# Gram lower triangles: four tiles loaded at once, two late, and the stores issued by ScalarE

## What is computed

```python
Z = jnp.einsum('bnd,bmd->bnm', inputs, inputs)
li, lj = jnp.tril_indices(64, k=-1)
return Z[:, li, lj]
```

## Time and profile before

| | before |
|---|---|
| median of 3 runs | 429.29 us |
| the profiled run | 430.24 us |
| its span | 428.5 us |
| TensorE matmul busy | 379.3 us |
| VectorE busy | 365.0 us |
| ScalarE busy | 177.9 us |
| GpSimd busy | 197.3 us |
| DMA, share of 16 engines' span | 92.8% |
| bytes read and written in HBM | 134.22 + 16.52 MB |
| mean granted TensorE clock | 0.979 |

### The profile page before, as it was taken

The page is one execution under the profiler, slowest core; times in us unless marked ns, Lnnn a source line. Parts: engine busy times, 40 slices in busy tenths (PEclk is TensorE's granted clock), DMA queues, the critical chain, the costliest instruction groups (busy, mean ns, idle before and its releaser), DMA issues.

```text
span 428.5 us, 68861 instructions
## 1 busy us (share of the span) xinstructions
PE 379.3 (89%) x33024; PEld 372.2 (87%) x33024; DVE 365.0 (85%) x224; ACT 177.9 (42%) x829; POOL 197.3 (46%) x980
## 2 busy tenths in 40 slices
PE   3529999999999999999999999999999998989900
PEld 3529999999999999999999999999999998989800
DVE  5316799999999999999999999999897979979734
ACT  0001213455335543455344543455444554344562
POOL 0000037281827465472808347182744728173584
PEclk9999999999999999999999999999999999999965
DMA  6699999999999999999999999999999999995416
GB/s 227 255 401 413 382 348 357 365 330 401 398 390 412 368 414 401 410 388 406 405 407 389 394 398 342 401 350 384 371 411 361 370 409 361 398 350 226 107 37 157
DMA packets 39610, 151.01 MB, mean 352 GB/s; under 512 B 4640, under 2 KB 4768, under 8 KB 39584
## 3 DMA queue, kind: packets, MB, share of 16 engines
q1 hardware_dynamic: 39584, 150.75, 92.8%
HBM read 134.22 MB, written 16.52 MB: 352 GB/s over the span
## 4 chain that ended last, share of the span: by engine, by line
PE 72%; SPq 11%; issue 6%; DMA 4%; POOL 3%; DVE 2%; ACT 0%; DVEq 0%; POOLq 0%; ACTq 0%
PE bank_set L264 72%; SPq L146 10%; DMA y_dram<-packed_rows 4%; POOL packed_rows L130 3%; SPq L151 1%; DVE packed_rows L130 1%; DVE row_halves L225 1%; DVE x_turned L231 0%; ACT products L291 0%; ACT packed_rows L125 0%; DVEq L67 0%; SPq L157 0%; DVEq L224 0%; POOLq L187 0%; ACTq L282 0%
## 5 line engine op out<-in xcount | busy, mean ns | idle before, releaser
L264 PE MATMUL bank_set<-x_turned 32*64 32x64 f32 x33024 | 379.3, 236 | 28.7 <-issue 18.2
L264 PEld LDWEIGHTS bank_set<-x_turned 32*64 32x64 f32 x33024 | 372.2, 132 | 35.6 <-issue 28.1
L208 DVE STREAM_TRANSPOSE x_turned<-x_in 128x2048 f32<-128x2048 f32 x128 | 292.0, 2290 | 49.2 <-PE bank_set L264 29.5
L130 POOL COPY packed_rows<-row_halves 32x60 f32<-32x60 f32 (+30 forms) x961 | 195.0, 205 | 224.7 <-DVE row_halves L225 100.2
L291 ACT COPY products<-bank_set 128x512 f32<-128x512 f32 (+1 forms) x91 | 68.6, 759 | 211.9 <-PE bank_set L264 192.5
L225 DVE STREAM_TRANSPOSE row_halves<-products 128x1024 f32<-128x1024 f32 x64 | 76.9, 1205 | 6.9 <-POOL packed_rows L130 5.3
L119 ACT COPY packed_rows<-row_halves 128x32 f32<-128x32 f32 (+30 forms) x481 | 62.8, 220 | 0.0
L125 ACT COPY packed_rows<-row_halves 128x128 f32<-128x128 f32 x256 | 57.0, 301 | 10.0 <-DMA y_dram<-packed_rows 7.8
L291 ACT ACT_TABLE_LOAD x1 | 1.3, 1283 | 20.6 <-PE bank_set L264 20.6
L130 DVE COPY packed_rows<-row_halves 32x2 f32<-32x2 f32 (+30 forms) x31 | 3.5, 191 | 0.0
L231 DVE MEMSET x_turned<- 128x2048 f32 x1 | 1.8, 1765 | 1.2 <-PEq L335 1.2
## 6 DMA issues: line engine op xcount, KB each, us to landing
x_in<-x_dram SPq DMA_DIRECT2D x256, 512.0 KB, 7.5
y_dram<-packed_rows SPq DMA_DIRECT2D x30, 504.0 KB, 7.3
y_dram<-packed_rows SPq DMA_DIRECT2D x2, 380.0 KB, 3.9
y_dram<-packed_rows SPq DMA_DIRECT2D x2, 124.0 KB, 3.9
```

The lines of the kernel that those rows point to most:

```text
L130: return copy(packed_rows[first:first + BLOCK, group % 2, :, at + BLOCK:at + i], row_halves[first + BLOCK:first + HALF, i, :, 0:i - BLOCK])
L208: nc.vector.transpose(x_turned[:, j].rearrange("p s c b (h u n v) -> p u v (s c b h) n", h=ROWS // BLOCK, u=PAIRS, v=PAIR), x_in[:, k].rea ...
L264: done = nc.tensor.matmul(bank_sets[s][side * HALF:(side + 1) * HALF, g, at, :].rearrange("r (n u v) -> r u n v", u=PAIRS, v=PAIR), rows, ...
```

## The change

Four edits:

1. Tiles 0 to 3 load without waits. Tile 4 waits until tile 0 has been multiplied, tile 5 until tile 1 has been. Tiles 6 and 7 follow in the queue, and from 8 on it is as before.
2. The stores of groups 0 to 14 are issued by ScalarE instead of SyncE: in the loop after a `keep`, once all 16 quarters of the group are packed, with the same waits; for group 14 after the loop, ahead of the first quarter of group 15. The two stores of group 15 stay with SyncE.
3. TensorE waits for the other set's `kept` ahead of the last two chunks of the last tile of each set: the wait for `kept[1]` moves from the start of `j` = 2 to near the end of `j` = 1. The wait for `kept[0]` stays where it was.
4. The tile of zeros is cleared half by VectorE (side 0), half by GpSimd (side 1).

```diff
-    APART = range(2, 5)
+    LATE = {4: 0, 5: 1}
@@ store, now with the engine as an argument
+        def store(engine, group, columns):
+            for side in range(SIDES):
+                first = group * GROUP + side * KEPT
+                engine.dma_start(y[first:first + KEPT, columns].rearrange("(h q) c -> q h c", q=BLOCK),
+                                 packed_rows[side * HALF:side * HALF + BLOCK, group % 2, :, columns]).then_inc(
+                    stored[group % 2], 16)
@@ sync
-                elif t in APART:
-
-                    sync.wait_ge(loaded[t - 1], SIDES * 16)
+                elif t in LATE:
+                    lap, j = place(LATE[t])
+                    sync.wait_ge(tile_multiplied[j], (lap + 1) * ARRAY_TILES)
...
             for t in range(TILES):
                 load(t)
-                group, behind = divmod(t - STORE_LAG, GROUP_TILES)
-                if group >= 0 and behind == 0:
-                    store_whole(group)
-            for group in range((TILES - 1 - STORE_LAG) // GROUP_TILES + 1, GROUPS - 1):
-                store_whole(group)
@@ gpsimd
             pool.sem_inc(kept[1], LAP)
+            for j in range(BLANK):
+                nc.gpsimd.memset(x_turned[:, j, 1:SIDES], 0.0).then_inc(turned[j], LAP - 1)
@@ vector
-                nc.vector.memset(x_turned[:, j], 0.0).then_inc(turned[j], LAP)
+                nc.vector.memset(x_turned[:, j, 0:1], 0.0).then_inc(turned[j], 1)
@@ tensor
                 s, in_set = set_of(j)
-                if s == 1 and in_set == 0:
-                    pe.wait_ge(kept[1], step)
...
-                        if j == LAP - 1 and slot == SLOTS - 1 and c == CHUNKS - 2:
-
-                            pe.wait_ge(kept[0], step)
+                        if in_set == SET_TILES[s] - 1 and slot == SLOTS - 1 and c == CHUNKS - 2:
+
+                            pe.wait_ge(kept[1 - s], step)
@@ scalar
+            def store_whole(group):
+                act.wait_ge(packed_home, (group + 1) * PIECES)
+                act.wait_ge(packed_across, (group + 1) * LONG_PIECES)
+                store(act, group, slice(0, PACKED))
+
             n = 0
+            stores = 0
             for lap in range(LAPS):
                 for s in range(SETS):
                     keep(lap, s)
+                    if n >= (stores + 1) * PIECES * 4:
+                        store_whole(stores)
+                        stores += 1
                     while n + PACK_LAG < (lap * LAP + (SET_TILES[0] if s == 0 else LAP) - BLANK) * 2:
                         pack(n)
                         n += 1
 
             for n in range(n, (GROUPS * PIECES - 1) * 4):
+                if n == (GROUPS - 1) * PIECES * 4:
+                    store_whole(GROUPS - 2)
                 pack(n)
```

More of the change, by code:

```diff
@@ L60, in gram_lower_triangle @@
     PACK_LAG = 2 * PIECE_LAG + 1
-    STORE_LAG = PIECE_LAG + 2 * PIECES + 3 + IN_RING
     STORES = SIDES * 16
@@ L171, in _ @@
             sync.wait_ge(last_carried, 1)
-            store(group, slice(long_rows, PACKED))
+            store(sync, group, slice(long_rows, PACKED))
             sync.wait_ge(packed_home, GROUPS * PIECES - 1)
             sync.wait_ge(last_packed, 1)
-            store(group, slice(0, long_rows))
+            store(sync, group, slice(0, long_rows))
             for b in range(2):
```

## The result

| | before | after |
|---|---|---|
| median | 428.72 us | 421.80 us (420.55 to 422.23) |
| ratio, 95% interval | | 0.9851 (0.9814 to 0.9889) |
| span of the profiled run | 428.5 us | 418.7 us |

The forecast was 424.0 us, 1.2% faster, in a range of 416 to 431.

The account below looks back on a forecast made before the run. The prediction took the DMA stream of loads and stores to bound the kernel from store 0 on. Span 428.5 less 1.4 (TensorE's end) and 3.9 (tail) gave 423.2, scaled to 424.0 us, range 416 to 431.

Parts of the forecast that it names:

- tile 31: Landing of this tile's load, around the first store: forecast at 102.9 us, against 102.4 before.
- the tail: Stretch from TensorE's end to the span's end: forecast at 16.6 us, 3.9 less than before, with ScalarE last.
- the loads' line: Loads and stores sharing the DMA, in order of time: forecast to set the end from store 0 on, 4.3 us a store.
- T1: Time at which TensorE has multiplied tile 1, in the start: forecast at 27.5 us (26.6 to 29.8) instead of 33.9.
- E: Time at which TensorE ends: forecast at 406.5 us against 407.94, 5.4 us after the last tile lands.
- its 397.5: TensorE's end in us if DMA did not bind: T1 + 9.8 + 41 x 8.785.
- The packet on an idle DMA: Third and fourth 16 KB code packets at the start, with no loads queued: 1.4 us after TensorE's restart (0.7 to 2.24).
- From tile 31 to tile 127: Middle stretch between these landings: twelve groups at 24.7 us, 296.4 us, plus 1.8, half of 3.7 for slower groups.
- rival 1: Stores on their own queue cost loads 3.6 us or less, so TensorE binds: median 414.9 us, chance 0.12.
- ScalarE's price: Cost of ScalarE issuing the stores in the middle: forecast 0, as a store may take 4.9 us there.
- Bank wait and zeros: Moved bank wait: 0; halved zeros: TensorE starts at 2.2 us (3.05 at worst), with the same T1.

Follow-up runs that it names:

- loads apart: The changed kernel with its first edit undone: tiles 2 to 4 load one after the other, tiles 5 to 7 without waits; 417.6 us, ratio 0.9761.

## Why the prediction was right, and where not

Profile against profile the change is 9.8 us: 0.5 up to tile 31, 6.6 from there to tile 127, 4.8 in the tail, less 2.1 that the last tiles gave back. With the second profile of the changed kernel it is 8.0 us: -0.3, 5.7, 4.7 and -2.1. The forecast was -0.5 + 1.9 + 3.9 = 5.3 us with nothing given back. So the forecast span of 423.2 us is 4.5 us above the first profile and 2.7 above the second, and 424.0 is 2.2 us above the median. In part that closeness is luck: the middle was forecast 4.7 us too long, and a loss of 2.1 us behind the last landing, which the forecast didn't have, took nearly half of that back.

**The bound.** Right. The claim that the loads' line decides from store 0 on, and that TensorE's early start is not won by it, is borne out three ways: with the stores back on SyncE the early start is worth nothing (1.0003); with the stores cut short TensorE ends 368.8 us after T1; with stores doubled the end moves by 3.6 us for each of 13. Where TensorE starts late enough it holds instead (the kernel before with ScalarE's stores, E = 403.4 against 402.7); the forecast had that bound as well, in its 397.5.

**The start.** T1 was forecast at 27.5 and was 26.8 and 27.6 us in two profiles. The packet on an idle DMA came 1.1 us after the restart, where I took 1.4 out of 0.7 to 2.24. The first restart was 9.69 (9.2), the second 14.79 (15.0), behind the end of the four loads. Tile 5 landed at 31.5 (32.3).

**Tile 31** landed at 101.9 (102.9), so that the late start was just paid by the time the ring used to be full. Right in the sum. What the forecast did not look at was whether the late start was needed: the same stores with loads apart are 2.9 us of span faster, 4.2 us by the medians.

**From tile 31 to tile 127.** The term that was mis-sized: 298.2 us forecast, 293.5 measured. I took 24.7 us a group from the kernel before, and half of its slower groups' 3.7 us on top. With the stores on ScalarE's queue a group takes 24.4 to 24.6 us on the mean (single groups 24.1 to 25.4, the first of the stretch aside). Eight profiles with ordinary stores on ScalarE's queue give 292.9 to 295.2 us for the stretch; three with stores behind the loads give 296.5, 297.8 and 300.1. The gain of a queue of its own is thus 0.1 to 0.6 us a group, not the 0.7 us a store and more that rival 1 asked for. The first of the twelve groups varies most (24.5 to 26.2 us); without it a group takes 24.4 to 24.5 us in the nine profiles with whole stores on ScalarE's queue and 24.7, 24.8 and 24.9 us in the other three. The pair that differs in the stores' queue alone (24.4 and 24.5 against 24.7) puts the gain at 0.2 to 0.3 us. Rival 1 was wrong as put (TensorE did not become the bound: E = 402.9, where T1 + 368.8 would be 395.6), but part of its gain is there. A store still costs the loads 24.46 - 8 x 2.53 = 4.2 us; tiles without a store land 2.51 to 2.56 us apart, which makes it 4.0 to 4.4.

The Trainium skill (DMA: Bandwidth & Descriptors, on issuing engines not being separate DMA queues) has it that only the sequencer's time is saved. The traces agree in the main: a store's price stays near 4.2 us on a queue of its own. The stretch as a whole is 1.3 to 7 us shorter there, and no run here says whether SyncE's time at issue makes that up.

**The last tiles.** Not in the forecast. I put E 5.4 us behind the last landing, as before. That holds where the last store stands just ahead of the last tile. On ScalarE's queue store 12 falls between tiles 121 and 122 (376.4 and 382.9 us); after it tiles land 2.5 us apart and TensorE needs 2.93, so E = 382.9 + 2.5 + 6 x 2.93 = 402.9, that is 7.5 us behind the last landing. It offset 2.1 us of the mis-sized middle. The waits also began earlier than forecast, at 220 instead of 250 us, and sum to 6.7 us (7.0 in the second profile) where 9 was forecast. That they begin early because a store's 4 us come in one piece, ahead of one tile, is argued and not tested.

**The tail.** 15.8 us against 16.6 forecast and 20.6 before. GpSimd is done with group 14 at E + 1.4 (E - 0.2 was forecast), near the tail's start. The forecast had ScalarE last, at E + 11.5, with 5.1 us behind it. It ends at E + 11.3, but taking its store away did not shorten the tail, so the bound is VectorE's last carry at E + 9.7 and four stores in a row behind it: from the first of the four to the span's end it is 6.0 us in the kernel before, in the changed one and in the one where SyncE issues store 14. Here the sum was near and its last link was wrong.

**ScalarE's price** in the middle was nothing, as forecast: two stores are issued in 0.81 us, and TensorE shows no wait for ScalarE. **Bank wait and zeros**: nothing with the late loads, as forecast. With loads apart they go together with 3.2 us (420.8 and 417.6 us), by the traces through the shift of the packets described above; the two were not tried singly.

## What to carry to other kernels

Where a ring of loads runs ahead, find out what a group of loads and stores takes by the landing of the same tile of each group, and set it against what the engine needs: a lead that shrinks slowly hides the true bound for most of the run. Stores that wait behind queued loads land late, and whoever waits for their buffer waits too: here that cost 4.8 us at the end. A second queue made a store at most some tenths of a microsecond cheaper but let the last ones go early, and where the last store falls among the last loads is worth microseconds. Before the start of a loop is cleared of loads to let its code in, check that the loads aren't what the rest of the kernel waits for.

## What the runs showed of the hardware

- A 16 KB packet of code for TensorE moved 1.1 us after a restart with nothing queued, and up to 4.5 us after one behind loads; TensorE resumed 2.2 to 2.6 us after the packet either way. With eight loads queued all gaps were 3.7 to 4.0 us.
- A store of 1.03 MB costs the loads' line 4.2 us, a second one right behind it 3.55, a 1.05 MB tile 2.53. Reading it from twice as many partitions changed nothing.
- Behind a full ring of loads stores 5 to 12 landed 17 to 18.5 us after issue (the changed start with SyncE's stores); on a queue of their own, 9 to 10 us.
- Two kernels with stores behind the loads spread most: 14 runs of the kernel before from 424.8 to 430.7 us, 10 with stores 0 to 11 there from 422.6 to 428.7. But ten runs with SyncE's stores and the changed start stay within 2.5 us (427.0 to 429.5), and with all stores on ScalarE's queue the spread is 1.6 to 3.1 us. So the place of the stores isn't shown to be the cause, and what plays there wasn't found.
